# A two-layer graph attention kernel: projections as half-array pairs, first score rows ahead of the masks, loop counts recovered from logarithms

## The reference, cut to what matters

```python
hv = h.reshape(n, 12, 64)                               # first layer: 12 heads of 64
ft = einsum('nhd,od->nho', hv, W);  res = einsum('nhd,od->nho', hv, W_res)
a1 = sum(ft * attn_l, -1);  a2 = sum(ft * attn_r, -1)
e = leaky_relu(a1[src] + a2[dst], 0.2)
w = exp(e - segment_max(e, dst)[dst])
agg = segment_sum(w / segment_sum(w, dst)[dst] * ft[src], dst)
x = layernorm(x + relu(agg + res))
...
# block 2: the edges again, with one more loop per node
h = gat_conv(x, edges + loops, W1, a_src1, a_dst1, b1, heads=4, out=256)
h = relu(layer_norm(h)) + (x @ Wr1 + br1)
h = gat_conv(h, edges + loops, W2, ..., heads=1, out=768);  h = layer_norm(h) + (h1 @ Wr2 + br2)
out = layernorm(x + h)
```

## Time and profile before

| | |
|---|---|
| median of 3 runs | 1151.51 us (1150.78 to 1153.05) |
| the profiled execution | 1150.89 us, of which the span from first to last instruction is 1148.9 |
| busy PE / DVE / ACT / POOL | 1061.3 / 974.4 / 646.4 / 145.9 us |
| counting | until 92.39 us |
| first attention layer's rows | about 100 to 460 us |
| second layer's products | about 460 to 650 us |

### The profile page before, as it was taken

How to read it: one execution, slowest core, us unless ns; L and a number is a source line. 1 busy time by engine, 2 the same in 40 slices (tenths; PEclk the granted TensorE clock), 3 DMA queues, 4 the chain that set the end, 5 groups by cost and what they waited for, 6 DMA issues and landing times.

```text
span 1148.9 us, 20069 instructions
## 1 busy us (share of the span) xinstructions
PE 1061.3 (92%) x7857; PEld 909.5 (79%) x7857; DVE 974.4 (85%) x1539; ACT 646.4 (56%) x1061; POOL 145.9 (13%) x154
## 2 busy tenths in 40 slices
PE   5997698989889898899999999999999999999996
PEld 3775466666656665799999999999998888888884
DVE  7998999999999999894884899999987874397874
ACT  7557699989999999322210467676722312234331
POOL 1000000000000000000056021120310133421111
PEclk9998899999999999999999999999999999999998
DMA  4114020202020203544046510203041124343211
GB/s 145 51 75 150 1 91 1 91 1 90 1 91 1 96 1 98 178 155 144 16 137 220 192 46 1 83 1 132 17 183 56 42 93 169 128 144 137 75 62 51
DMA packets 39860, 98.95 MB, mean 86 GB/s; under 512 B 4467, under 2 KB 17147, under 8 KB 39765
## 3 DMA queue, kind: packets, MB, share of 16 engines
q1 hardware_dynamic: 39766, 97.66, 24.7%
HBM read 70.74 MB, written 26.90 MB: 85 GB/s over the span
## 4 chain that ended last, share of the span: by engine, by line
PE 60%; DVE 27%; issue 10%; DMA 1%; ACT 1%; POOL 0%; DVEq 0%; SPq 0%; POOLq 0%
PE psum L1027 14%; DVE R L1555 14%; PE psum L938 13%; PE psum L988 12%; PE psum L1056 9%; DVE R L1541 7%; PE psum L953 4%; PE psum L717 3%; PE psum L821 2%; PE psum L1004 1%; DVE LC L1524 1%; PE psum L1039 1%; PE psum L809 1%; DVE stats L1563 1%; DMA rowbuf<-rows_spill 0%
## 5 line engine op out<-in xcount | busy, mean ns | idle before, releaser
L880 PE MATMUL psum<-ident,R 128*128 128x128 f32 (+3 forms) x1200 | 159.5, 282 | 48.7 <-ACT R L1175 48.5
L880 PEld LDWEIGHTS psum<-ident,R 128*128 128x128 f32 (+3 forms) x1200 | 129.7, 143 | 89.8 <-ACT R L1175 82.0
L1555 DVE CUSTOM_DVE_ANT_0 R<-R,LC 128x1250 f32<-128x1250 f32 x120 | 173.1, 1443 | 0.0
L1175 ACT ACTIVATE R<-R,row_max 128x1250 f32<-128x1250 f32 x120 | 161.3, 1344 | 12.6 <-DVE row_max L1555 10.8
L894 PE MATMUL psum<-R 128*64 128x256 f32 (+3 forms) x1200 | 148.2, 386 | 0.0
L1191 ACT COPY R<-psum 128x1280 f32<-128x1280 f32 x120 | 143.2, 1194 | 1.5 <-PE psum L880 1.5
L938 PE MATMUL psum<-w_hi,x1T_hi 128*128 128x256 f32 (+1 forms) x480 | 136.4, 284 | 3.8 <-DVE x1T_lo L1635 1.6
L938 PE MATMUL psum<-w_lo,x1T_hi 128*128 128x256 f32 (+1 forms) x480 | 135.1, 282 | 0.0
L938 PE MATMUL psum<-w_hi,x1T_lo 128*128 128x256 f32 (+1 forms) x480 | 135.1, 281 | 0.0
L1541 DVE SCALAR_TENSOR_TENSOR R<-R 128x1250 f32<-128x1250 f32 x80 | 120.4, 1505 | 0.0
L2004 POOL TENSOR_TENSOR rstd<-rstd,minus_half 128x1 f32<-128x1 f32 (+1 forms) x40 | 32.5, 812 | 686.8 <-DVE rstd L1568 686.8
(11 more groups left out here) (220 smaller groups left out, 2533.8 us busy)
## 6 DMA issues: line engine op xcount, KB each, us to landing
R<-rows_spill SPq DMA_DIRECT2D x20, 625.0 KB, 5.5
rowbuf<-rows_spill SPq DMA_DIRECT2D x14, 625.0 KB, 5.2
lc_spill<-LC SPq DMA_DIRECT2D x9, 625.0 KB
LC<-lc_spill SPq DMA_DIRECT2D x9, 625.0 KB, 5.5
res_spill<-colbuf SPq DMA_DIRECT2D x36, 128.0 KB, 2.5
R<-res_spill SPq DMA_DIRECT2D x9, 512.0 KB, 4.0
R<-in_x_dram SPq DMA_DIRECT2D x1, 3456.0 KB
res_spill<-R SPq DMA_DIRECT2D x9, 384.0 KB
```

What stands on the lines that cost most here:

```text
L880: last = e.transpose(turn0[r % 2][0:m, s, 0:n_dst], ring[0:n_dst, r % RING0, s * P:s * P + m], ident[0:n_dst, 0:n_dst])
L1175: e.activation(ring[0:m, r % RING0, :], ring[0:m, r % RING0, :], ACT.Exp, bias=row_max[0:m, r % RING:r % RING + 1], scale=-1.0, accum_out= ...
L1555: e.tensor_tensor_reduce(slot, slot, LC[0:m, i, :], -1.0, MIN_CEILING, ALU.add, ALU.min, row_max[0:m, r % RING:r % RING + 1]).then_inc(S.l ...
```

## The change

It has three parts. (1) The projections become 20 chunks of three pairs; in each pair, partitions 0 to 63 (one head) and 64 to 127 (the other) of the array take one product of 130 columns each, into two banks. The chunks are put among counting segments 18 to 54 instead of 18 to 64 (`LAST_COUNTS` 4 to 14), and the score rows' turning moves with them. ScalarE copies a chunk with three instructions. (2) `count_loops` is gone; the logarithms no longer wait for it, and a table load is put at the start. VectorE starts `leaky0(0)` and `leaky0(1)` ahead of the first mask; masks 5, 4 and 3 come one row earlier or in one go, and the PSUM fills come behind them. (3) The loops' counts are taken back from the diagonal of `LC`: VectorE reads each diagonal block's greatest entry (`loop_logarithm`, behind `dots1(10)` to `(19)`), ScalarE takes the exponential behind p = 32, VectorE rounds in two steps, ScalarE takes the logarithm behind p = 42. `one_more_edge` starts at p = 50 and has one operation a tile, and POOL holds 24 of its 40 additions until that is done.

```diff
-        CONST_ZERO, CONST_IOTA, CONST_EARLY, CONST_RHS = 1, 2, 11, 12
+        CONST_ZERO, CONST_IOTA, CONST_EARLY = 1, 2, 12
+        def proj_psum(c):
+            return psum[:, 6:8, 0:KG * PROJ] if c % 2 else psum[:, 2:4, 0:KG * PROJ]
-        DOTS1_EARLY, LC1_FROM = 24, 52
+        DOTS1_EARLY, LC1_FROM, B1_HELD = 24, 50, 16
+        LOOPS_EXP, LOOPS_LN = 32, 42
-        W_COUNTS, FIRST_COUNTS, TURN_COUNTS, LAST_COUNTS = 3, 8, 18, 4
+        W_COUNTS, FIRST_COUNTS, TURN_COUNTS, LAST_COUNTS = 3, 8, 18, 14
...
-                    e.matmul(side_bank(use)[0:m, 0:2 * P + 4], xT[:, k, i * P:i * P + m], rhs[:, k, :],
-                             start=True, stop=True).then_inc(S.ft_sum, 1)
+            for c in range(2 * NT):
+                i, g = divmod(c, 2)
+                m = rows[i]
+                done = count_until(done, TURN_COUNTS + c * (COUNTS - LAST_COUNTS - TURN_COUNTS) // (2 * NT))
+                if c >= 2:
+                    e.wait_ge(S.ft, c - 1)
+                for j in range(KG):
+                    k = g * KG + j
+                    for half in range(2):
+                        ps = slice(half * C0, half * C0 + C0)
+                        last = e.matmul(proj_psum(c)[0:m, half, j * PROJ:(j + 1) * PROJ], xT[ps, k, i * P:i * P + m],
+                                        rhs[ps, k, :], start=True, stop=True)
+                last.then_inc(S.ft_sum, 1)
...
-                    done = count_until(done, COUNTS - 1)
+                    done = count_until(done, COUNTS - LAST_COUNTS + 1 + piece)
...
+            e.preload_act_table(ACT.Ln)
...
-                e.wait_ge(S.diag, s + 1)
...
+                if p == LOOPS_EXP:
+                    e.wait_ge(S.diag, NT)
+                    e.activation(diag_count[:, :], diag_count[:, :], ACT.Exp).then_inc(S.diag_exp, 1)
+                if p == LOOPS_LN:
+                    e.wait_ge(S.diag_round, 2)
+                    e.activation(diag_ln[:, :], diag_count[:, :], ACT.Ln, bias=2.0, scale=2.0).then_inc(S.diag_ln, 1)
+                    e.preload_act_table(ACT.Exp)
...
-            for k in reversed(range(NT)):
-                count_loops(k)
...
-            mask(NT - 1)
             e.wait_ge(S.terms0, 1)
             leaky0(0)
+            leaky0(1)
+            mask(NT - 1)
             mask(NT - 2)
-            leaky0(1)
             least0(0)
             mask(NT - 3)
-            mask_at = {1: (NT - 4,), 2: (NT - 5,), 3: (NT - 6, NT - 7), 4: (NT - 8,), 5: (NT - 9,), 6: (NT - 10,)}
+            mask_at = {1: (NT - 4,), 2: (NT - 5, NT - 6, NT - 7), 4: (NT - 8,), 5: (NT - 9,), 6: (NT - 10,)}
             for r in range(ROWS0):
                 if r in mask_at:
                     for k in mask_at[r]:
                         mask(k)
+                if r == 2:
+                    e.wait_ge(S.lc_ln, TURNS)
+                    for b in range(2):
+                        e.memset(turn0[b][96:P, NT - 1, :], 0.0).then_inc(S.terms0, 1)
                 if r + 2 < ROWS0:
                     leaky0(r + 2)
                 if r + 1 < ROWS0:
                     least0(r + 1)
-                if r == 0:
-                    e.wait_ge(S.lc_ln, TURNS)
-                    for b in range(2):
-                        e.memset(turn0[b][96:P, NT - 1, :], 0.0).then_inc(S.terms0, 1)
...
+            def loop_logarithm(k):
+                m = rows[k]
+                if k:
+                    e.wait_ge(S.diag, k)
+                e.tensor_tensor_reduce(junk_loop[0:m, 0:m], LC[0:m, k, k * P:k * P + m], loop_only[0:m, 0:m], 1.0, MAX_FLOOR,
+                                       ALU.add, ALU.max, diag_count[0:m, k:k + 1]).then_inc(S.diag, 1)
+
             for p in range(DOTS1_EARLY):
                 dots1(p)
                 if p == 9:
                     rest_w1(WBUFS1 + 1)
+                if p > 9 and p - 10 < NT:
+                    loop_logarithm(p - 10)
+            e.wait_ge(S.diag_exp, 1)
+            e.tensor_scalar(diag_count[:, :], diag_count[:, :], 0.5, WHOLE, ALU.mult, ALU.add).then_inc(S.diag_round, 1)
+            e.wait_ge(S.diag_round, 1)
+            e.tensor_scalar(diag_count[:, :], diag_count[:, :], -WHOLE, None, ALU.add).then_inc(S.diag_round, 1)
...
-                e.tensor_tensor(block_, block_, off_diag[0:m, 0:m], ALU.mult).then_inc(S.lc1, 1)
-                e.wait_ge(S.lc1, 2 * i + 1)
-                e.scalar_tensor_tensor(out=block_, in0=ident[0:m, 0:m], scalar=diag_ln[0:m, i:i + 1], in1=block_,
-                                       op0=ALU.mult, op1=ALU.add).then_inc(S.lc1, 1)
+                e.scalar_tensor_tensor(out=block_, in0=loop_only[0:m, 0:m], scalar=diag_ln[0:m, i:i + 1], in1=block_,
+                                       op0=ALU.add, op1=ALU.max).then_inc(S.lc1, 1)
...
             for p in range(XLS1):
+                if p == B1_HELD:
+                    e.wait_ge(S.lc1, NT)
                 add_b1(p)
```

More of the change, by code:

```diff
@@ L190, in gnn_kernel @@
         attnT = view(R2, NT * D + 3 * P, [2 * H0], F32, C0)
-        rhs = view(rows_flat, 0, [KT, 2 * P + 4])
+        PROJ, KG = 2 * C0 + 2, KT // 2
+        rhs = view(rows_flat, 0, [KT, PROJ])
+        assert KG * PROJ <= BANK
         ring = view(R1, 0, [RING, N])
@@ L1113, in act_program @@
             e.wait_ge(S.w_turned, 1)
-            e.wait_ge(S.const, CONST_RHS)
             e.copy(attnT, bank[0:C0, 0:2 * H0]).then_inc(S.attnT, 1)
[L1116 to L1120, removed]
-            last.then_inc(S.rhs_w, 1)
+            e.copy(rhs[:, :, 0:C0], bank[:, P:P + C0].unsqueeze(1).to_broadcast([P, KT, C0]))
+            e.copy(rhs[:, :, C0:2 * C0], bank[:, 2 * P:2 * P + C0].unsqueeze(1).to_broadcast([P, KT, C0])).then_inc(S.rhs_w, 1)
             bank = side_bank(1)
@@ L1125, in act_program @@
                 ps = slice(half * C0, half * C0 + C0)
-                for part in range(2):
-                    last = e.copy(rhs[ps, :, 2 * P + 2 * part + half],
-                                  bank[ps, part * H0 + half:(part + 1) * H0:2])
+                last = e.copy(rhs[ps, :, 2 * C0:2 * C0 + 2],
+                              bank[ps, 0:2 * H0].rearrange("p (s k h) -> p k s h", s=2, h=2)[:, :, :, half])
             last.then_inc(S.rhs, 1)
@@ L1511, in dve_program @@
             e.drain().then_inc(S.counted, 1)
-            def count_loops(k):
-                m = rows[k]
-                if k < NT - 1:
-                    e.wait_ge(S.diag, NT - 1 - k)
-                e.tensor_tensor_reduce(colbuf[0:m, 0:m], CT[0:m, k, k * P:k * P + m], ident[0:m, 0:m], 1.0, 0.0,
-                                       ALU.mult, ALU.add, diag_count[0:m, k:k + 1]).then_inc(S.diag, 1)
             def mask(k):
@@ L1992, in pool_program @@
                             pattern=[[-1, P]], channel_multiplier=1).then_inc(S.const, 1)
[L1993 removed]
+            e.affine_select(out=loop_only[:, :], in_=loop_only[:, :], compare_op=ALU.not_equal, fill=0.0, base=0,
                             pattern=[[-1, P]], channel_multiplier=1).then_inc(S.const, 1)
@@ L1998, in pool_program @@
             e.memset(tiny[:, :], LN_TINY).then_inc(S.const, 1)
-            e.memset(rhs[:, :, :], 0.0).then_inc(S.const, 1)
+            e.memset(diag_count[:, :], 0.0).then_inc(S.const, 1)
             def norm_power(v, i):
```

49 lines of the change are left out of this document (21 added, 28 removed).

## The result

| | before | after |
|---|---|---|
| median | 1151.78 us (1150.78 to 1153.05, 4 runs) | 1162.05 us (1161.17 to 1163.42, 4 runs) |
| ratio after / before | | 1.0086, 95% interval 1.0072 to 1.0099 |
| profiled execution's span, mean granted clock | 1148.9 us, 0.983 | 1160.7 us, 0.975 |

The changed kernel is slower by 0.86%; 1161.6 us were forecast. The total is right, its four terms are each off by 1 to 4 us, and the errors cancel in part. I go through the profile in the order of time.

A forecast was written before the change was run, and what follows sets the result against it. Bounds: VectorE (barely) in counting, TensorE in the second layer's products. Terms -0.5 - 2.5 + 11.6 + 1.7 = +10.3 us gave 1161.2 on the profiled execution, 1161.8 on the median; forecast 1161.6, range 1158 to 1171.

The forecast's parts named there:

- clock behind it: Second layer's products, after the stall: TensorE's clock at the lower level loses 1.7 us, bounds 0.9 to 2.5.
- step 1: Counting: projections as pairs keep TensorE's period at 4.15 us, under VectorE's 4.41; -0.5 us, bounds -1.3 to +8.
- the fast end: Counting: pairs run side by side, loads included, so a chunk costs 0.94 us instead of 1.46 with single-file loads.
- steps 2 and 3: Ahead of the first layer: early score rows and uncounted loops free 6.7 us, 2.5 gained after new waits; bounds 1.5 to 3.5.
- step 4: Second layer's products: ScalarE waits for the tenth loop logarithm at 567.0 us, so TensorE stands 11.6 us before product 37.
- lower bound, 10.5: Second layer's products: the stall in us if a logarithm fills the gaps between dot products.
- Step 5: Table loads, a logarithm, rounds, fewer edge operations and POOL's held additions: costed at nothing, bounds 0 to +3 us.
- Rival C: Second layer's products: tenth logarithm ready before TensorE runs out of banks at 555.4 us, no stall; 1148.5 us, chance 0.07.
- B: Counting: weight loads go single file, counting ends 8 us later; 1170 us, or 1166 halfway; chance 0.30.
- D: First layer's new waits eat the front gain and POOL's held additions reach TensorE: +2.5 and +3, 1167 us; chance 0.05.

The follow-up runs named there:

- 4: The kernel before with only the projections as pairs, chunks among segments 18 to 54 (`LAST_COUNTS` 14): 1153.71 us, ratio 1.0008.
- 6: Kernel 1 with the projections' pairs put among the counting segments one by one instead of three at a time: 1152.61 us, ratio 1.0004.
- 9: Kernel 1 with `LAST_COUNTS` 10 instead of 14, one chunk behind every second counting segment: 1148.11 us, ratio 0.9965.
- 1: The changed kernel with ScalarE's wait for the loops' logarithms behind product 36 instead of 32: 1150.19 us, ratio 0.9983.
- 7: Kernel 1 with VectorE's two PSUM fills ahead of masks 5, 4, 3 instead of behind them: 1149.04 us, ratio 0.9973.
- 11: Kernel 1 with `LAST_COUNTS` 4 instead of 14, so the score rows are turned at the end of counting again: 1155.63 us, ratio 1.0029.
- 2: The changed kernel with ScalarE's wait for the loops' logarithms behind product 34 instead of 32: 1157.32 us, ratio 1.0037.
- 3: The changed kernel with the ten logarithms behind dot products 0 to 9 instead of 10 to 19: 1151.39 us, ratio 0.9988.
- 5: The kernel before with only the projections as pairs, chunks among segments 18 to 64 (`LAST_COUNTS` 4): 1152.82 us, ratio 1.0004.
- 8: Kernel 1 with POOL no longer holding 24 of its 40 bias additions: 1151.12 us, ratio 0.9985.
- 10: The changed kernel with wait behind product 36, fills ahead of masks 5, 4, 3, and `LAST_COUNTS` 10: 1146.47 us, ratio 0.9948.

## Why the prediction was right in sum and wrong in its terms

| term | forecast | the profiled execution after | settled by |
|---|---|---|---|
| counting | -0.5 | +1.6 | 4, 6, 9 |
| score rows, masks, fills | -2.5 | -1.1 (125.31 - 124.79, less 1.6) | 1, 7, 11 |
| from there to product 32 | 0 | +0.9 (549.46 - 548.00, less 0.5) | 1, 2, 3: scatter |
| stall | +11.6 | +7.7 | 1, 2, 3 |
| clock behind it | +1.7 | +2.7 | 2 |
| sum | +10.3 | +11.8 (the spans: 11.8) | |

The errors are +2.1, +1.4, +0.9, -3.9 and +1.0 us. That the sum came out within 1.5 of the profiled execution, and nearer still to the median, is partly luck.

*Counting (step 1) failed.* The price of a chunk was close (1.01 for 0.94 us), and the choice of the fast end, for the rows where two halves alternate, was right. What failed is to compare the period's average with VectorE's 4.41 us: 20 chunks in 36 segments fall as two or three to a period, and one with three takes 2.06 + 3.03 = 5.09. That is 0.9 us of the waits; the other 0.6 come from chunks between the two segments of a group that VectorE wants 1.84 us after the last (kernels 5, 9, 11). Kernel 9, which has neither, has the gain that I had forecast, and 0.6 more.

*The front (steps 2 and 3) was right where the clock is full.* With a full clock (kernel 1) VectorE left counting at 93.66, 1.27 later than before, and reached the mask of 124.79 at 123.54, 1.25 earlier: 2.5 us gained in between, the forecast number. In the changed kernel's own profile 1.4 of them went to the clock between 100 and 104 us. I had not seen that with TensorE's work moved forward its clock may fall behind it. It does not always: of the profiled executions with `LAST_COUNTS = 14` those of after, 3 and 8 lost it at the end of counting, those of 1, 2, 4, 6 and 7 didn't; with 10, kernel 10 had it at the lower level from 98 to 100 us and kernel 9 did not; the three with 4 kept it. What decides between them stays open.

*The stall (step 4) was right in mechanism and place, and its term was mis-sized.* The price of a logarithm was taken from a queue where nothing else stands between them, 0.32 us; between dot products it is 0.02. The lower bound, 10.5, was meant for just this case, and took only a third of it off: with 1.03 us from tile to tile the tenth is ready at 563.8, and the same sum gives a stall of 8.4. In full: the tenth came 10.4 us behind dot product 10, not 13.5; dot product 10 itself was 1.1 later (554.55 for 553.45); so TensorE went on at 565.69 and not at 567.8, 2.1 earlier. And it ran dry 1.8 later than the 556.2 that I took from the kernel before, since the products were 1.46 late. 2.1 and 1.8 are the 3.9 us between 11.6 and 7.7.

*The clock* cost 2.7 us rather than 1.7. The windows above make 10.2 us at the lower level (each one's shortfall from 1.00, doubled, times its length); 4.8 of them passed in the idle itself, up to 565.7, the rest, 5.4, on TensorE's work, at half its pace. In kernel 2, with 3.5 us of idle, 2.5 were lost. So it isn't the length of the idle that made 1.7 too small: behind 3.5 us and behind 7.7 us it cost nearly the same, as I had assumed, but more than behind the 3.9 us at 112 us that I had read it from, where TensorE worked 3.4 us at the lower level. Why the clock came back sooner there stays open.

*Step 5* stands: table loads, rounds, edge operations and the held additions cost nothing that the runs show (kernels 1 and 8). Rival C's mechanism is real, and kernel 3 bears out its condition: with the tenth logarithm there before TensorE is out of banks, nothing stops; as the change was made, it came 8 us too late for that (565.0 against 555.4 + 1.5 = 556.9). Rivals B and D are out.

*The 0.9 us between the masks and product 32* are scatter of single executions, as far as the traces go. 0.43 of it is a wait of VectorE for TensorE at 149 us, behind a stretch at the lower clock (142 to 148 us, granted clock 0.51) that the kernel before did not have. But kernels 1, 2 and 3 have the same instructions in the same order up to product 32's copy, but for the places of the logarithms in kernel 3, and from the mask to that copy they take 422.2, 422.8 and 422.8 us; the kernel before took 423.2 (548.00 - 124.79) and the changed kernel 424.2.

## What to carry to other kernels

When an engine's wait is put into another engine's stream, count what that stream still feeds: a wait is free up to the moment at which its consumers run out of buffers, and from there costs its full length and the clock behind it. Here that was a matter of four places in a list, and 12 us. Work that is interleaved with a full engine must fit where it stands, in every period and before the next result that the other engine wants; the average does not tell. One number that put 20 chunks between whole groups, one behind every second segment, was worth 2 us, and the same work in finer pieces cost 2.4, as each change of the array costs 0.35. Price a small operation between the neighbours that it will really have.

## What the runs showed of the hardware that was not expected

- Half-array passes of 64 rows with 128-column loads, half of them on each of the two row halves, follow each other after 0.055 us, loads included. On each half that is one after 0.11 us, where two loads on one half of the array were 0.105 apart: no half is quicker than it was, but the two work side by side without a loss that shows. The Trainium skill's TensorE: Matmul & The Clock Gate, LDWEIGHTS, puts a load's time down to its columns whatever its rows; the trace agrees, for each half by itself.
- Changing the array from whole to halves and back costs 0.35 us, with 12 passes between or with 4 and 8; it is what remains when the passes are taken off.
- Executions of one kernel differ in where TensorE's clock falls. Whether this is what spreads their times is not shown: among the 12 runs of kernel 1 the span went from 1146.3 us at a mean clock of 0.989 to 1151.9 at 0.978, but one with 0.979 took 1147.7, and among the 10 runs of kernel 9 and the 29 of the kernel before there is no such relation.
